# Sum of squares as two fp32r products, and one copy moved ahead of a Gelu

## The reference, cut to what matters

```
ctx      = causal_ema(x);  wg = sigmoid([x, ctx] Wg + bg);  gated = x * wg
h1       = gelu(x Wn1 + bn1);  mod = 0.5 + sigmoid(h1 Wn2 + bn2)
temporal = sum over d of blend[d] * causal_ema(gated * mod[d])
gate     = sigmoid(temporal Wtemp + btemp);  soma = gelu(x Wsoma + bsoma)
out      = (soma * gate) Wout
result   = (out - mean(out)) / sqrt(var(out) + 1e-5) * gamma + beta
```

## Time and profile before

| | |
|---|---|
| median of 3 runs (lowest, highest) | 1363.86 us (1363.69, 1365.89) |
| the profiled execution | 1364.18 us |
| its span, first to last instruction | 1362.5 us, so 1.7 us lie around it |
| PE busy | 1353.7 us, 99% |
| DVE busy | 779.8 us, 57% (eight or nine tenths in the slices from 820 us on) |
| ACT busy | 481.2 us, 35% |
| PE in the chain that ended last | 93% |
| mean granted TensorE clock | 1.000 |

### The profile page before, as it was taken

The page is one execution under the profiler, slowest core; times in us unless marked ns, Lnnn a source line. Parts: engine busy times, 40 slices in busy tenths (PEclk is TensorE's granted clock), DMA queues, the critical chain, the costliest instruction groups (busy, mean ns, idle before and its releaser), DMA issues.

```text
span 1362.5 us, 15161 instructions
## 1 busy us (share of the span) xinstructions
PE 1353.7 (99%) x5912; PEld 1105.8 (81%) x5912; DVE 779.8 (57%) x1035; ACT 481.2 (35%) x799; POOL 134.6 (10%) x170
## 2 busy tenths in 40 slices
PE   9999999999999999999999999999999999999998
PEld 7888888888888888888887887878787878787877
DVE  4335243333252332342221586999999989898994
ACT  5444233332242432332321223243424342424253
POOL 5000100000100000100000221012101220032000
PEclk9999999999999999999999999999999999999999
DMA  5523433502532412631322945621232123212101
GB/s 134 140 70 116 125 107 123 155 16 101 139 121 80 154 43 87 165 109 46 101 78 86 210 158 193 163 89 62 93 124 94 62 94 124 93 63 93 47 16 62
DMA packets 68375, 140.89 MB, mean 103 GB/s; under 512 B 7328, under 2 KB 19616, under 8 KB 64336
## 3 DMA queue, kind: packets, MB, share of 16 engines
q1 hardware_dynamic: 61360, 116.71, 27.8%
q0 software_dynamic: 6944, 23.23, 5.7%
HBM read 86.85 MB, written 53.05 MB: 103 GB/s over the span
## 4 chain that ended last, share of the span: by engine, by line
PE 93%; DVE 4%; DMA 1%; issue 1%; ACT 0%; POOL 0%; SPq 0%; DVEq 0%; POOLq 0%
PE bank L990 31%; PE bank L991 31%; PE bank L992 31%; DVE drive L1423 1%; DMA x_slot<-x2hl_dram 1%; DVE drive L1408 1%; PE bank L1057 1%; DVE temporal L1433 0%; PE bank L1165 0%; DVE temporal L1423 0%; DMA mod_t<-mod_dram 0%; DMA x_raw<-in_x 0%; DVE spikes_lo L1267 0%; ACT temporal L840 0%; DVE gated L1392 0%
## 5 line engine op out<-in xcount | busy, mean ns | idle before, releaser
L1267 DVE TENSOR_TENSOR h_hl<-bank,h_hl 128x512 fp32r<-128x512 f32 x128 | 88.7, 693 | 465.9 <-ACT h_hl L862 465.9
L990 PE MATMUL bank<-x_hl,wa 128*128 128x512 f32 x512 | 199.7, 390 | 0.9 <-DVE x_hl L1267 0.9
L992 PE MATMUL bank<-x_hl,wa 128*128 128x512 f32 x512 | 199.2, 389 | 0.0
L991 PE MATMUL bank<-x_hl,wa 128*128 128x512 f32 x512 | 199.2, 389 | 0.0
L992 PE MATMUL bank<-h_hl,wa 128*128 128x512 f32 x512 | 199.2, 389 | 0.0
L990 PE MATMUL bank<-h_hl,wa 128*128 128x512 f32 x512 | 199.2, 389 | 0.0
L991 PE MATMUL bank<-h_hl,wa 128*128 128x512 f32 x512 | 199.2, 389 | 0.0
L858 ACT ACTIVATE bank<-bank,small_sb 128x512 f32<-128x512 f32 x128 | 84.2, 658 | 212.2 <-PE bank L992 212.1
L862 ACT ACTIVATE h_hl<-bank 128x512 fp32r<-128x512 f32 x128 | 76.7, 599 | 228.5 <-PE bank L992 228.0
L990 PEld LDWEIGHTS bank<-x_hl,wa 128*128 128x128 f32 x512 | 96.1, 188 | 23.1 <-DVE x_hl L1267 1.7
L992 PEld LDWEIGHTS bank<-x_hl,wa 128*128 128x128 f32 x512 | 96.2, 188 | 20.0
(11 more groups left out here) (163 smaller groups left out, 2315.9 us busy)
## 6 DMA issues: line engine op xcount, KB each, us to landing
x_slot<-x2hl_dram SPq DMA_DIRECT2D x32, 513.0 KB, 4.7
x2hl_dram<-x_hl POOLq DMA_DIRECT2D x28, 512.0 KB, 9.1
stage<-in_l_w SPq DMA_DIRECT2D x32, 256.0 KB, 3.1
x_dram<-x_raw SPq DMA_DIRECT2D x8, 1024.0 KB, 5.6
xt<-x_dram SPq DMA_DIRECT2D x8, 1024.0 KB, 5.7
mod_t<-mod_dram POOLq DMA_DIRECT2D x8, 1024.0 KB, 5.0
x_raw<-in_x SPq DMA_DIRECT2D x7, 1024.0 KB, 9.3
out<-y_sb SPq DMA_DIRECT2D x28, 256.0 KB, 2.3
```

The lines of the kernel that those rows point to most:

```text
L990: eng.matmul(ps, w_hi, x_hi, start=first, stop=False)
L991: eng.matmul(ps, w_hi, x_lo, start=False, stop=False)
L992: return eng.matmul(ps, w_lo, x_hi, start=False, stop=final)
L1267: return eng.tensor_tensor(lo, raw, hi.bitcast(F32), ALU.subtract)
```

## The change

The tile `sumsq` is split like the other operands. ACT copies it to fp32r (`sumsq_hi`) into the last chunk of `ts_hi`, which is free then; DVE subtracts (`sumsq_low`) in place; and `ss` becomes two fp32r matmuls with ones, one waiting for the high part and one for the low part. The last tile (i = 7) keeps the plain fp32 product. `sumsq_hi(r-1)` stands on ACT ahead of `soma_of(r, 0)`; in round 1 it stands behind `wg_tanh(1, 3)`. `sumsq_low(r-1)` stands on DVE between the gated and the drives of the last chunk; in round 1 it stands right behind `scan_g(1, 3)` and ahead of `traces_c(1, 2)`. Apart from that, `temporal_hi(r-1, 3)` is moved ahead of `h1_of(r)` in rounds 2 to 7, and it also waits for the `ss` that reads the chunk of `ts_hi`.

```diff
+        sumsq_lo = place("sumsq_lo", 30, [TOK], F32R)
-        ones = const("ones", P)
+        ones = const("ones", P, F32R)
...
             def temporal_hi(i, m):
                 on.wait_ge(s_add, SH * (KC * i + m + 1))
                 if i:
                     on.wait_ge(s_pe["OU"], KC * i)
+                    if m == KC - 1:
+                        on.wait_ge(s_pe["SS"], i)
...
+            def sumsq_hi(i):
+                on.wait_ge(s_ssq, SH * (i + 1))
+                eng.activation(ts_hi[:, KC - 1, :], sumsq[:, :], ACT.Copy).then_inc(s_ssqhi, 1)
...
             wg_tanh(1, 3)
+            sumsq_hi(0)
             soma_of(1, 0)
...
             for r in range(2, NT):
+                temporal_hi(r - 1, 3)
                 h1_of(r)
-                temporal_hi(r - 1, 3)
                 mod_of(r)
...
                 o_of(r - 1, 3)
+                sumsq_hi(r - 1)
                 soma_of(r, 0)
...
             def ss(i):
                 on.wait_ge(s_cst, 1)
                 on.wait_ge(s_sq, KC * i + 1)
-                on.wait_ge(s_ssq, SH * (i + 1))
-                eng.matmul(SS_BANK[:, :], ones[:, :], sumsq[:, :], start=True, stop=True).then_inc(s_pe["SS"], 1)
+                if i == LAST:
+                    on.wait_ge(s_ssq, SH * (i + 1))
+                    eng.matmul(SS_BANK[:, :], ones[:, :].bitcast(F32), sumsq[:, :], start=True, stop=True
+                               ).then_inc(s_pe["SS"], 1)
+                    return
+                on.wait_ge(s_ssqhi, i + 1)
+                eng.matmul(SS_BANK[:, :], ones[:, :], ts_hi[:, KC - 1, :], start=True, stop=False)
+                on.wait_ge(s_ssqlo, i + 1)
+                eng.matmul(SS_BANK[:, :], ones[:, :], sumsq_lo[:, :], start=False, stop=True
+                           ).then_inc(s_pe["SS"], 1)
...
+            def sumsq_low(i):
+                on.wait_ge(s_ssqhi, i + 1)
+                low_part(sumsq_lo[:, :], sumsq[:, :], ts_hi[:, KC - 1, :]).then_inc(s_ssqlo, 1)
...
             sum_squares(0)
             scan_g(1, 3)
+            sumsq_low(0)
             traces_c(1, 2)
...
                 sum_squares(r - 1)
-                traces_a(r, 3)
+                gated_of(r, 3)
+                sumsq_low(r - 1)
+                drive_of(r, 3, 0)
+                drive_of(r, 3, 1)
                 traces_b(r, 3)
```

More of the change, by code:

```diff
@@ L211, in build @@
         s_ssq = sem("s_ssq")
+        s_ssqhi = sem("s_ssqhi")
+        s_ssqlo = sem("s_ssqlo")
         s_std = sem("s_std")
@@ L1195, in _ @@
             for _ in range(12):
-                eng.matmul(bank[7][:, 0:P], ones[:, :], ones[:, :], start=True, stop=True)
+                eng.matmul(bank[7][:, 0:P], ones[:, :].bitcast(F32), ones[:, :].bitcast(F32), start=True, stop=True)
             for u in range(UNITS + 2):
@@ L1501, in x3_low @@
                          ).then_inc(s_x3lo, n)
-            eng.memset(ones[:, :], 1.0)
+            eng.memset(ones[:, :].bitcast(F32), 1.0)
             eng.memset(eps_sb[:, :], 1e-5).then_inc(s_cst, 1)
```

## The result

The changed kernel takes 1372.4 us in the median of 6 runs (1370.99 to 1374.13), the kernel before 1364.69 us beside it (1363.69 to 1366.13): a ratio of 1.0057, 95% interval 1.0046 to 1.0068, so 7.7 us slower. The profiled execution took 1370.99 us, the shortest of the six, with a span of 1369.3 us, 6.8 us more than the one before.

What follows compares the result with a forecast made beforehand. PE, busy 99% of the span, was taken as the bound. +7.5 at mo(2), -0.3 at te(1, 0), -2.05 in rounds 2 to 6 and +0.75 in round 7 make +5.9: 1369.8 us as median, range 1366.6 to 1373.8.

Steps and rivals of the forecast that it cites:

- rival 1: PE clock falls to 1.2 GHz in the stall at mo(2): 2.7 us more, 1372.5 us; chance 0.25.
- The head of round 2: Moved copy waits for tile 1's last add ahead of the Gelu: mo(2) 7.5 us later, 5.3 of it new stall.
- The 0.3 us given back at te(1, 0): te(1, 0) had waited 0.3 to 0.4 us for DVE; its low parts are now ready before, so -0.3 us.
- ss(0): In round 1 the split's parts come late: PE 2.2 us late, DVE 2.0 us late.
- Rounds 2 to 6: Two fp32r products replace the plain one with parts in time: 0.41 us saved per round, 2.05 us in all.
- a later round shorter by more than 0.5 us: Sign that the prediction is wrong: any later round shorter than before by more than 0.5 us.
- Round 7: DVE's subtraction is not covered between its first drive and te(7, 0): +0.75 us on the end.
- the lead from the move ends at mod_t: At the head of round 7, DVE's lead of 2.6 us ends in a longer wait for mod_t.
- the forecast's likeliest case: The stall costs its own length alone, without a clock fall: 1369 to 1370.6 us; chance 0.53.
- Rivals 2 and 4: 2: tile 1's last add early enough, 1364.5 us, chance 0.07; 4: products with ones cost 0.43 us each, 1371.8, chance 0.04.
- Rival 3: Round 7: mod_t(7) lands after 5.0 us rather than 6.8, about 2.7 us less, 1367.1 us; chance 0.08.
- The wait at ss(0): Sign expected in the profile after: PE's wait at ss(0) is near 2.5 us.

Runs made afterwards that it cites:

- busy_at_all_waits: Changed kernel plus unused fp32r products at PE's three waits: 8 at ss(0), 22 at mo(2), 8 at te(7, 0); 1369.53 us, ratio 1.0035.
- before_kept_busy: Kernel before plus 8 unused fp32r products where PE waits for te(7, 0); 1364.26 us against 1364.16, ratio 0.9999.
- split_tiles_0_to_5: Kernel before with sumsq split for tiles 0 to 5 and the copy ahead of the Gelu in rounds 3 to 7 only; 1365.17 us, ratio 0.9999.
- h1_first_in_round2: Changed kernel with the Gelu ahead of the copy again in round 2 alone; 1365.52 us, ratio 1.0008 to the kernel before.
- busy_in_the_stall: Changed kernel plus 22 unused fp32r products ahead of mo(2); 1371.22 us, ratio 1.0046 to the kernel before.
- move_only: Kernel before with the copy moved ahead of the Gelu in rounds 2 to 7, sumsq not split; 1372.3 us, ratio 1.0062.
- use_the_lead: Kernel before with tiles 1 to 5 split, copy moved in rounds 3 to 7, round 7's x3_low subtractions before DVE's first drive, spikes before first scan; 1360.96 us.
- use_the_lead_again: Same kernel as use_the_lead, measured again beside reorder_without_the_move on the same chip; 1361.05 us, ratio 0.9970 to the kernel before.
- reorder_without_the_move: As use_the_lead, but with the Gelu ahead of the copy in every round; 1361.0 us, ratio 0.9969 to the kernel before.

## Why the prediction held, and where it was off

The forecast of 1369.8 us is 2.6 below the measured median. The terms of its sum held one by one; the range held because it took in rival 1, which came true.

- **The head of round 2** was the term that decided. mo(2) was forecast 7.5 us late, with a stall of 5.3; the table has 159.74 - 152.31 = 7.4, and the wait is 5.33. Shown by putting the two lines back (-6.9 us) and by the move alone (+7.7). The 0.3 us given back at te(1, 0) are 0.24: from mo(2) to te(1, 0) it takes 5.43 us before and 5.19 in busy_at_all_waits.
- **ss(0)**, 2.2 us on PE and 2.0 on DVE: the product after the pair starts at 883.49 instead of near 881.8, and mo(0) of that trace stands 0.5 us earlier, so 2.2. The copy at the head of round 2 starts at 897.53 instead of 896.05, so DVE is 2.0 late by the same count. Alone the split of tile 0 cost 1.9 us, a lower clock included.
- **Rounds 2 to 6**, 5 x 0.41 = 2.05: the pair saves 0.42 in the trace, and the step from mo(2) to mo(7) falls from 352.86 to between 350.4 and 351.4 us in the eight traces that split these tiles and have neither a lowered clock in that step nor the stall ahead of it, 1.5 to 2.4 us. Both parts are in time, as worked out: no wait at these five. One of the prediction's signs of being wrong was set too near its own saving, a later round shorter by more than 0.5 us: counted from mo to mo, rounds 3, 4 and 5 take 69.91, 69.96 and 69.99 us instead of 70.44, 70.47 and 70.75, so 0.5, 0.5 and 0.8 less. 0.41 of that is the split; the rest is within what these rounds differ by between traces (before_kept_busy: 70.59, 70.53 and 70.39).
- **Round 7**, +0.75: the step from the first drive to te(7, 0) grew by 0.67: the subtraction takes 0.69. That the lead from the move ends at mod_t is shown by the two kernels without the move.
- **The clock** is what the forecast's likeliest case had wrong. It took "the waits so far left the clock alone" from one profile, and gave the fall a chance of 0.25. It fell in all six runs, whose mean clock is 0.996 to 0.998. The sum without it, +5.9, is what busy_at_all_waits measured, and the rest up to 7.7 us, 1.8, is what the clock costs the changed kernel beyond what it costs the kernel before, whose runs are a mixture. Rival 1, with 2.7 for the stall's fall, came true with its size too high. In the trace, the 4.1 us at 0.50 behind the stall lose half of that, some 2.0 us, and in both this trace and that of busy_at_all_waits mo(2) starts at 898.8, but te(1, 0) at 905.84 and 903.97: 1.9 us. Falls at ss(0) and te(7, 0) come on top in some runs. And the premise was false for the kernel before as well: on the chip of split_tiles_0_to_5 12 of its 29 runs had 1.000 and a median of 1363.86 us, 13 had 0.998 and 1365.74, and 4 had 0.999 and 1365.04. The profile shown was one of the first kind. The Trainium skill (TensorE: Matmul & The Clock Gate, "HAM oscillation — how this bites in real kernels") describes matmuls that start at the lower clock behind a wait, and the trace agrees for the stall: 0.50 behind 5.33 us. That single waits of 1.9 us were also followed by 0.51 is what these traces add.
- Rivals 2 and 4 did not occur: the copy behind the last add started at 897.53, later than before, and the products with ones cost 0.23 us each. Rival 3 did not either: mod_t(7) landed after 6.9 us, not 5.0, and PE waits 1.85 us at te(7, 0), as before. The wait at ss(0), expected near 2.5 us, is 2.1.

## What to carry to other kernels

A step moved ahead of another on an in-order engine must be costed in every round of the loop that holds it: five rounds had room for the copy, the sixth made nearly the whole regression. Where the bounding engine stands still, count the clock after it as well as the wait, and read the granted clock of every run, not of the one profile. A faster product is only worth its place where its operands are ready: splitting five tiles of seven gained 1.3 to 1.6 us, and tile 0 on top gave it back, in part through the clock.

## What was not expected of the hardware

The clock fell behind waits of 1.9 us in some executions and not in others. Runs of the same kernel differ in their mean clock, and the traces show where: behind te(7, 0) in h1_first_in_round2 and not in the changed kernel, behind ss(0) in busy_in_the_stall and split_tiles_0_to_5 and not in h1_first_in_round2. One such fall at te(7, 0) costs 1.6 us: from te(7, 0) to the end the traces without it take 51.8 us (before: 622.9 - 571.12) and those with it 53.4 (move_only: 632.5 - 579.08). With the wait at 1.4 or 1.5 us all 20 runs stayed at 1.000 (use_the_lead, use_the_lead_again, reorder_without_the_move); their traces also lack the wait at ss(6) that the kernel before and all other kernels with split tiles show, 0.2 to 1.2 us, so it isn't shown that the shorter wait is the reason. What decides between executions stays open.
